# AdaLN, a selective scan and a mixture of experts in one kernel: fewer ScalarE and VectorE instructions per scan state, two more buffers, loads dealt out over other steps

## The reference, cut to what matters

```python
mod = (silu(c) @ wmod).reshape(4, 6, 1, 512)        # sa, ca, ga, sb, cb, gb; |ga|, |gb| kept >= 0.25
h = layernorm(x) * (1 + ca) + sa
x = x + ga * mamba(h)
h = layernorm(x) * (1 + cb) + sb
x = x + gb * moe(h)

def mamba(x):                                        # D = 512 channels, N = 16 states
    val, gate = split(x @ W_in)
    val   = silu(conv3(val))                         # depthwise, 3 taps
    Delta = softplus((val @ W_delta + delta_base) @ W_tau)
    dA    = Delta[..., None] * (-exp(A_log))
    A_bar = exp(dA)
    B_bar = expm1(dA) / (dA + 1e-6) * Delta[..., None] * (val @ W_B)[:, :, None, :]
    h_t   = A_bar_t * h_{t-1} + B_bar_t * val_t      # scan over the tokens
    y_t   = sum_n h_t * C_t                          # C = val @ W_C
    return (y * silu(gate)) @ W_out + x

def moe(x):                                          # 8 experts, hidden 256, top 2, and a shared one
    g = top2_normalized(sigmoid(x @ gate_W) * route_scale)
    return sum_e g_e * (gelu(x @ W1_e + b1_e) @ W2_e + b2_e) + shared(x)
```

## Time and profile before

| what | value |
|---|---|
| median of 3 runs | 4806.98 us (4793.49 to 4813.43) |
| the profiled execution | 4803.95 us, its span 4802.2 us |
| busy, share of the span | PE 81%, VectorE (DVE) 85%, ScalarE (ACT) 83%, GpSimd (POOL) 76% |
| mean share of the DMA engines' time: SyncE's queue, GpSimd's queue | 46.6%, 28.5% |

### The profile page before, as it was taken

The page is one execution under the profiler, slowest core; times in us unless marked ns, Lnnn a source line. Parts: engine busy times, 40 slices in busy tenths (PEclk is TensorE's granted clock), DMA queues, the critical chain, the costliest instruction groups (busy, mean ns, idle before and its releaser), DMA issues.

```text
span 4802.2 us, 37156 instructions
## 1 busy us (share of the span) xinstructions
PE 3874.3 (81%) x9708; PEld 1621.0 (34%) x9708; DVE 4088.0 (85%) x4054; ACT 4003.3 (83%) x4510; POOL 3648.1 (76%) x2308
## 2 busy tenths in 40 slices
PE   6623514989898888989898988899898977989889
PEld 3211201333333333333343333333333333333344
DVE  1398899999999999999999999999998998788830
ACT  1687889998999998999989998989899997978811
POOL 0399978887888888888878887888888886767621
PEclk8856756999999999999999999999999987989889
DMA  4678857878787978788787878887887885667542
GB/s 136 210 227 260 255 130 218 232 219 254 227 254 218 264 216 260 226 245 241 224 248 225 247 222 257 231 247 226 241 252 217 240 225 148 183 166 194 155 135 66
DMA packets 352222, 1037.19 MB, mean 216 GB/s; under 512 B 41254, under 2 KB 44390, under 8 KB 344711
## 3 DMA queue, kind: packets, MB, share of 16 engines
q1 hardware_dynamic: 278282, 766.35, 46.6%
q0 software_dynamic: 73728, 268.47, 28.5%
HBM read 639.74 MB, written 126.51 MB: 160 GB/s over the span
## 4 chain that ended last, share of the span: by engine, by line
PE 26%; ACT 23%; issue 15%; DVE 12%; DMA 12%; POOL 10%; SPq 0%; POOLq 0%; DVEq 0%; ACTq 0%
DMA ysum<-hs 9%; PE ps L1103 7%; PE ps L1122 6%; ACT inv L761 4%; PE ps L1073 3%; POOL inv L1377 3%; ACT inv L755 3%; DVE ps L1163 3%; DVE ps L1171 2%; DVE ps L1157 2%; ACT th L769 2%; ACT inv L766 2%; DVE hs L1191 2%; ACT abar L773 2%; PE ps L1047 2%
## 5 line engine op out<-in xcount | busy, mean ns | idle before, releaser
L1377 POOL TENSOR_TENSOR inv<-inv,th 128x1024 f32<-128x1024 f32 x512 | 1253.5, 2448 | 314.5 <-ACT th L769 314.4
L1103 PE MATMUL ps<-hf,w1r 128*128 128x512 f32 x2304 | 1115.0, 637 | 68.7 <-ACT xn L871 23.8
L1350 POOL TENSOR_TENSOR hs<-hs,Cb 128x1024 f32<-128x1024 f32 x384 | 962.3, 2506 | 54.0 <-DVE hs L1191 37.3
L1140 PE MATMUL ps<-Brow,pick 48*128 48x512 bf16 x1024 | 347.0, 423 | 593.4 <-DVE hs L1191 593.0
L1122 PE MATMUL ps<-w2r,hid 128*128 128x512 f32 x1776 | 816.1, 606 | 1.7 <-ACT xn L871 1.7
L1157 DVE TENSOR_TENSOR ps<-ps,us 128x1024 f32<-128x1024 f32 x512 | 628.3, 1227 | 193.7 <-PE ps L1140 193.3
L769 ACT ACTIVATE th<-delta,halfA 128x1024 f32<-128x1024 f32 (+1 forms) x640 | 606.3, 966 | 139.4 <-POOL inv L1377 139.3
L1191 DVE TENSOR_TENSOR_SCAN hs<-abar,carry,ps 128x512 f32<-128x512 f32 (+1 forms) x384 | 683.7, 1802 | 32.1 <-DMA ysum<-hs 32.0
L1171 DVE SCALAR_TENSOR_TENSOR ps<-ps,coef,inv 128x1024 f32<-128x1024 f32 (+1 forms) x640 | 674.3, 1072 | 25.9 <-POOL inv L1377 2.3
L1180 DVE SCALAR_TENSOR_TENSOR ps<-nrd,inv_kappa,ps 128x1024 f32<-128x1024 f32 (+1 forms) x640 | 675.3, 1073 | 16.1
L755 ACT ACTIVATE inv<-nrd,kappa 128x1024 f32<-128x1024 f32 (+1 forms) x640 | 577.0, 968 | 132.2 <-DVE ps L1171 132.1
(11 more groups left out here) (155 smaller groups left out, 5081.5 us busy)
## 6 DMA issues: line engine op xcount, KB each, us to landing
ysum<-hs POOLq DMA_DIRECT2D x512, 512.0 KB, 5.4
Cb<-c_rows SPq DMA_DIRECT2D x384, 512.0 KB, 4.5
w1r<-in_W SPq DMA_DIRECT2D x144, 512.0 KB, 5.5
w2r<-w_scaled SPq DMA_DIRECT2D x141, 512.0 KB, 6.7
Cb<-c_rows SPq DMA_DIRECT2D x128, 256.0 KB, 3.9
gbc<-expert_gates SPq DMA_DIRECT2D x128, 256.0 KB, 5.2
aw<-in_W_val SPq DMA_DIRECT2D x64, 256.0 KB, 6.0
xa<-in_x SPq DMA_DIRECT2D x32, 512.0 KB, 7.8
```

Source lines behind the costliest of these rows:

```text
L1103: mm = t.matmul(o, w1r[:, n % 2, k, h * P:(h + 1) * P], hf[:, k, :], start=(k == 0), stop=(k == G - 1))
L1350: gp_.tensor_tensor(hs[:, c % 3, :], hs[:, c % 3, :], Cb[:, c % 2, :], ALU.mult).then_inc(hC_done, 1)
L1377: gp_.tensor_tensor(inv[:, c % 6, :], inv[:, c % 6, :], th[:, c % 2, :], ALU.mult).then_inc(thinv_done, 1)
```

## The change

It (1) joins the four logarithms of a batch to two over [128, 2048], with the guard as a number in place of a column; (2) moves the coefficient of `times_weight` into the Exp of the inverse as a bias per partition (its logarithm), so that this Exp becomes two instructions in units of two halves while `times_weight` becomes one, with 1.0 as scalar; (3) writes `times_u` as a scalar_tensor_tensor; (4) takes the reciprocal standard deviations as Ln and Exp with a scale of -0.5 on ScalarE, at the places where these tables are already loaded, and drops Sqrt and reciprocal; (5) gives `hs` and `aw` a fourth buffer; (6) does the front's normalization, its statistics and transposes some steps earlier; (7) evicts two Delta products (`take_p` 2 and 3) in front of `times_ratio` at r = 11; (8) deals the loads of W2 (one expert a step: 12, 13, 15; 24, 25, 26; 30, 31, 0), W1 (7, 9; 25), h (r = 1), the aw weights and the h store (r = 29) over other steps. The last block keeps whole groups of W2.

```diff
-    AWB = 3
+    AWB = 4
-        hs = sb("hs", [P, 3, TB])
+        hs = sb("hs", [P, 4, TB])
...
-                done(v.reciprocal(coef[:], absA))
+                done(v.tensor_scalar(ln_coef[:], alog.rearrange("p g n -> p n g"), -2.0, math.log(DA_EPS), ALU.mult, ALU.add))
...
-            def load_w2(q, grp):
+            def load_w2(q, grp, members=(0, 1, 2)):
...
-                for p in GROUPS[grp]:
+                for p in [GROUPS[grp][m] for m in members]:
...
-            if r == 31:
-                load_aw(qn, 3)
...
+            if r == 2:
+                load_aw(qa, 7)
...
+            if r in (12, 13, 15) and qf != NQ - 1:
+                load_w2(qf, 0, ((12, 13, 15).index(r),))
             if r == 5:
-                load_w2(qf, 0)
                 if qf == NQ - 1:
+                    load_w2(qf, 0)
                     load_w2(qf, 1)
...
-            if r == 7:
-                load_aw(qa, 7)
+            if r in (7, 9):
+                load_w1(qf, (r - 7) // 2)
+            if r == 8:
                 load_aw(qa, 8)
-                load_w1(qf, 0)
-                load_w1(qf, 1)
-            if r == 8:
                 load_aw(qa, 9)
+            if r == 9:
                 load_aw(qa, 10)
-            if r == 9:
                 load_aw(qa, 11)
...
-            if r in (12, 17) and has(qn):
-                part = r // 17
+            if r in (12, 13) and has(qn):
+                part = r - 12
...
-            if r == 23:
-                load_w2(qf, 2 if qf == NQ - 1 else 1)
-            if r == 24:
+            if r == 23 and qf == NQ - 1:
+                load_w2(qf, 2)
+            if r in (24, 25, 26) and qf != NQ - 1:
+                load_w2(qf, 1, (r - 24,))
+            if r == 25:
                 load_w1(qf, 8)
...
-                    sp.wait_ge(st_h, 16 * (qx + 1))
-                    sp.dma_start(hf[:], h_d[qx]).then_inc(h_ld, 16)
+            if r == 1 and has(qf):
+                ge(sp, mm_w1, 2 * EX * qf)
+                sp.wait_ge(st_h, 16 * (qf + 1))
+                sp.dma_start(hf[:], h_d[qf]).then_inc(h_ld, 16)
             if r == 30:
                 load_gate_row(qf, 7)
-                if qf != NQ - 1:
-                    load_w2(qf, 2)
-            if r == 31:
+            if r == 29:
                 if has(qn):
                     sp.wait_ge(ev_t, G * (qn + 1))
                     sp.dma_start(h_d[qn], hTv).then_inc(st_h, 16)
+            if r in (30, 31) and qf != NQ - 1:
+                load_w2(qf, 2, (r - 30,))
+            if r == 0 and qp != NQ - 1:
+                load_w2(qp, 2, (2,))
...
-            def log(c):
-                act.wait_ge(sq_done, c + 1)
-                s.activation(inv[:, c % 6, :], inv[:, c % 6, :], ACT.Ln, bias=consts[:, 1:2]).then_inc(ln_done, 1)
+            def logs(c):
+                act.wait_ge(sq_done, c + 2)
+                two = flat(inv[:, c % 6:c % 6 + 2, :])
+                s.activation(two, two, ACT.Ln, bias=INV_GUARD).then_inc(ln_done, 2)
...
-                s.activation(inv[:, c % 6, :], inv[:, c % 6, :], ACT.Exp, scale=-1.0).then_inc(inv_done, 1)
+                for cols, g in parts(u):
+                    ins = s.activation(inv[:, c % 6, cols], inv[:, c % 6, cols], ACT.Exp, scale=-1.0,
+                                       bias=ln_coef[:, c % N, g:g + 1])
+                ins.then_inc(inv_done, 1)
...
             if w == 2:
-                if place == "start" and has(qf):
+                if place == "half logs" and has(qf):
                     act.wait_ge(f_stat, (TPB + 1) * (qf + 1))
-                    s.activation(rstdF[:, :, 0], momF[:, :, 1], ACT.Sqrt, bias=consts[:, 0:1]).then_inc(f_sqrt, 1)
+                    s.activation(rstdF[:, :, 0], momF[:, :, 1], ACT.Ln, bias=consts[:, 0:1]).then_inc(f_log, 1)
+                if place == 0 and has(qf):
+                    act.wait_ge(f_log, qf + 1)
+                    s.activation(rstdF[:, :, 0], rstdF[:, :, 0], ACT.Exp, scale=-0.5).then_inc(f_rstd, 1)
...
             if w == 5:
+                if place == "half logs" and has(qn):
+                    act.wait_ge(a_stat, (TPB + 1) * (qn + 1))
+                    s.activation(rstdA[:, :, 0], momA[:, :, 1], ACT.Ln, bias=consts[:, 0:1]).then_inc(a_log, 1)
+                if place == 0 and has(qn):
+                    act.wait_ge(a_log, qn + 1)
+                    s.activation(rstdA[:, :, 0], rstdA[:, :, 0], ACT.Exp, scale=-0.5).then_inc(a_rstd, 1)
             if w == 6:
                 if place == "start":
                     take_w1(qf, 6)
-                    if has(qn):
-                        act.wait_ge(a_stat, (TPB + 1) * (qn + 1))
-                        s.activation(rstdA[:, :, 0], momA[:, :, 1], ACT.Sqrt, bias=consts[:, 0:1]).then_inc(a_sqrt, 1)
...
-                if place == "squared" and has(qn):
+                if place == "squared":
+                    take_t(qn, (0, 1))
+                if place == "logs":
+                    take_t(qn, (2, 3))
+            if w == 5:
+                if place == 1 and has(qn):
                     act.wait_ge(a_rstd, qn + 1)
...
-                24: [("w1", qf, 13), ("w1", qf, 14)], 25: [("w1", qf, 15)], 26: [("w1", qf, 16), ("w1", qf, 17)],
-                27: [("t", qn, 0), ("t", qn, 1), ("w2", qf, 4)], 28: [("w2", qf, 5), ("t", qn, 2), ("t", qn, 3)], 29: [("w2", qf, 6)],
+                24: [("w1", qf, 13), ("w1", qf, 14)], 25: [("w1", qf, 15)] + [("t", qn, g) for g in range(G)], 26: [("w1", qf, 16), ("w1", qf, 17)],
+                27: [("w2", qf, 4)], 28: [("w2", qf, 5)], 29: [("w2", qf, 6)],
...
-                    v.tensor_tensor(X(c), X(c), us[:, u % 2, :], ALU.mult).then_inc(uB_done, 1)
+                    v.scalar_tensor_tensor(X(c), X(c), 1.0, us[:, u % 2, :], ALU.mult, ALU.mult).then_inc(uB_done, 1)
...
-                    for cols, g in parts(u):
-                        ins = v.scalar_tensor_tensor(X(c)[:, cols], X(c)[:, cols], coef[:, c % N, g:g + 1], inv[:, c % 6, cols],
-                                                     ALU.mult, ALU.mult)
-                    ins.then_inc(pw_done, 1)
+                    v.scalar_tensor_tensor(X(c), X(c), 1.0, inv[:, c % 6, :], ALU.mult, ALU.mult).then_inc(pw_done, 1)
...
-                    if c >= 3:
-                        dve.wait_ge(y_summed, 16 * (c - 2))
+                    if c >= 4:
+                        dve.wait_ge(y_summed, 16 * (c - 3))
...
+                if r == 11:
+                    take_p(qa, 2)
+                    take_p(qa, 3)
...
-                if r == 21 and has(qn):
+                if r == 16 and has(qn):
                     dve.wait_ge(ax_ld[0], 16 * (qn + 1))
                     tile_stats(xa, statsA, a_stat, (0, 1))
-                if r == 22 and has(qn):
+                if r == 17 and has(qn):
```

More of the change, by code:

```diff
@@ L1 @@
 from contextlib import ExitStack
+import math
 import numpy as np
@@ L97, in adaln_mamba_moe @@
         inv_kappa = sb("inv_kappa", [P, N, G])
-        coef = sb("coef", [P, N, G])
+        ln_coef = sb("ln_coef", [P, N, G])
         delta_lo = sb("delta_lo", [P, G])
         tau_bias = sb("tau_bias", [P, G])
-        consts = sb("consts", [P, 2])
+        consts = sb("consts", [P, 1])
         modc = sb("modc", [P, MODS * G, NB])
@@ L614, in sync_steps @@
             if r == 11:
-                load_aw(qn, 0)
-                load_aw(qn, 1)
-                load_aw(qn, 2)
+                for j in range(AWB):
+                    load_aw(qn, j)
             if r == 13:
@@ L801, in act_batch @@
             at("squared")
-            for c in states[0:2]:
-                log(c)
+            if states:
+                logs(c0)
             at("half logs")
-            for c in states[2:4]:
-                log(c)
+            if states:
+                logs(c0 + 2)
             at("logs")
@@ L953, in act_steps @@
                     ins.then_inc(a_xn, 1)
-                if place == 3:
-                    take_t(qn, (0, 1))
             if w == 7:
                 if place == "start":
-                    take_t(qn, (2, 3))
                     gelu(qf, 2)
@@ L986, in bank_held_to @@
                 return at + 1.95
-            held = {"t": (28.7, 28.7, 29.5, 29.5), "val": (1.5, 2.5, 3.5, 3.9), "gate": (8.3, 8.4, 9.5, 9.6), "p": (10.9, 11, 11.4, 11.5),
+            held = {"t": (26, 26.1, 26.4, 26.5), "val": (1.5, 2.5, 3.5, 3.9), "gate": (8.3, 8.4, 9.5, 9.6), "p": (10.9, 11, 11.4, 11.5),
                     "bc": (14.6,), "t2": (12, 12.1, 12.6, 12.7), "log": (14.95,), "gT": (15.9,),
@@ L1219, in mean_and_variance @@
                 ins.then_inc(sm, 1)
-            def rstd_of(rstd, sm):
-                v.reciprocal(rstd[:, :, 0], rstd[:, :, 0]).then_inc(sm, 1)
             def add_x1(kind, q, i, done, taken_):
@@ L1288, in late @@
                     take_p(qa, r - 9)
-                if r == 11:
-                    take_p(qa, 2)
-                    take_p(qa, 3)
-                if r == 25 and has(qn):
```

(9 more changed lines are left out.)

19 lines of the change are left out of this document (8 added, 11 removed).

## The result

The changed kernel takes 4858.89 us (median of 4 runs, 4855.09 to 4861.69), the kernel before 4806.91 us on the same chip: a ratio of 1.0109 (95% interval 1.0096 to 1.0121). It is 1.1% slower, where 4699 us was forecast. The profiled execution's span is 4858.3 us. Further down, one execution of e7 took 6053 us at a granted clock of 0.62, where its three others took 4698 to 4700 us at 0.89; it is left out of e7's number.

What follows compares the result with a forecast made beforehand. VectorE was taken as the bound, with three engines close behind. Savings of 41 + 40 + 45 less 35 us of new waits gave 91, plus 12 + 5 at the ends: 108 us off, so 4699 us, range 4635 to 4785.

Steps and rivals of the forecast that it cites:

- late loads: Rival: three late loads make TensorE wait some 4 us each, 12 us a window; slower, 4842 us; chance 0.07.
- the wait for B: VectorE waiting for TensorE's spread of B, twelve middle windows: 45 of 86.7 us would go, mainly at steps 27 and 28.
- VectorE's own work: Twelve middle windows: `times_weight` 29.6 us, `times_u` 7.3 and dropped reciprocals 3.9 less, together 41 us.
- the wait for y: VectorE's scan waiting for y's addition, middle windows: a fourth `hs` would remove 40 of 48.9 us.
- VectorE's waits for ScalarE and GpSimd: Middle windows: half of a 5.7 us a window difference in shrinkage taken as new VectorE waits, 35 us, bounds 0 and 70.
- Loads ... that cover it, and I cost it at nothing: Three loads one step ahead of use: TensorE waits 0 to 2 us, covered by its lead on VectorE; cost nothing.
- point of decision: The late-load rival was said to decide from some 3 us of TensorE waiting at each load.
- The objection to it: Against the late-load rival: W1, W2 and h are no longer sent in bursts of 1.5 to 2 MB.
- The table load: On ScalarE: a load costs 1.3 us by the trace; the skill's added 1380 ns drain was left out of the sum.
- `times_weight`: On VectorE: without its scalar column, 1285 ns becomes 1208, 77 ns a state, 29.6 us over 384 states.
- `times_u`: On VectorE: the new form goes from 1227 to 1208 ns, 7.3 us over 384 states.
- The logarithms: On ScalarE: two of 1137 ns become one of 1911, saving 363 ns each, 69.7 us over 192.

Runs made afterwards that it cites:

- e7: Changed kernel with W2 groups 1 and 2 loaded whole at steps 23 and 30, last W1 at 23, experts' deviation as before: 4698.40 us, 0.9786 of the kernel before.
- e1: Changed kernel with only the last expert's W1 load moved back from step 25 to step 24: 4818.07 us, 1.0027 of the kernel before.
- e11: e1 with group 1 of W2 loaded whole at step 23, group 2 still ending at step 0: 4819.81 us, 1.0027 of the kernel before.
- e2: e1 with W2 group 1 loaded whole at step 23 and group 2 whole at step 30: 4758.75 us, 0.9901 of the kernel before.
- e5: e2 with the experts' deviation as before, Sqrt at the start of batch 2 and a VectorE reciprocal: 4709.42 us, 0.9806 of the kernel before.
- e10: Changed kernel, late loads included, with only the experts' deviation back to Sqrt and reciprocal: 4802.06 us, 1.0000 of the kernel before.
- e6: e2 with the last expert's W1 loaded at step 23 instead of 24: 4752.17 us, 0.9893 of the kernel before.

## Why the prediction was wrong, step by step

The forecast gave 82% to faster and 7% to the rival that came true. That rival, late loads, was worked out at 4842 us; measured are 4859. It was at hand with its place and its price, and was turned down for a reason that does not hold.

The term of the sum that carried the failure is the wait for B. For the 384 states of the middle the forecast took 45 us off it; in the changed kernel it went from 86.7 to 195.7 us, 109 more. VectorE's own work fell by 32 us there (41 forecast), the wait for y by 48.9 (40), and VectorE's waits for ScalarE and GpSimd rose by 2 (35): late loads and a late deviation both reach VectorE as a late B.

**The step that failed: "Loads ... that cover it, and I cost it at nothing".** It set a landing time of 6.7 us against a step of 8.3 us, counted from the step in which the load stands in the program. But a queue in program order issues a load when it gets there. The changed kernel's trace has W1 issued at the moment at which TensorE is free for it (2058.38 and 2058.25), so the whole flight is waited for. Two of the three loads named cost 41 us (W1 at 25, e1) and 61 us (W2 at 0, e11 to e2); the third, W2 at 26, costs nothing (e11). The rows of before could have shown it: there W1, issued a step earlier, was already waited for 13 times, 20.9 us in all, and a step of advance taken from a load that is late is a step of waiting. The rival was right in kind and by parts in size: behind 3957 us it had +36 us, measured are 35, but for the middle its terms come to +11 us (57 + 35 - 41 - 40) and measured are 30. Its point of decision, some 3 us at each load, was passed at W1 alone (6.79 us here); for W2 at step 0 the changed kernel's TensorE waits 18.4 us in the middle stretch, 1.5 a window, and 3.3 once W1 is earlier (40.0 in e11). The objection to it, that smaller bursts land faster, was true and beside the point: the median w1r lands in 5.1 us where it took 5.5, w2r in 5.5 where it took 6.7, and the late W1 in 6.0 to 6.6 where it took 7.6 to 9.5.

**The second: new waits for ScalarE and GpSimd, taken at 35 us.** The text named the right place, GpSimd's normalization and all that queues behind it, but priced it as half of a balance between two engines' busy times. Nothing in that balance knows of an instruction order. It costs 49 to 57 us by itself (e5, e10), from 7.25 us of GpSimd idle a window (87.0 / 12), and little of it shows as VectorE waiting for ScalarE or GpSimd. The order of the program and durations like those in the earlier trace rows were enough to see it: a joined logarithm and a block of 1.9 us each, two table loads of 1.28 and three instructions of 1.13 to 1.15 us, that overlap a little, stand between the two small ones, 9.5 us in all.

**What was right.** With these edits mended, e7 takes 4698.40 us, the forecast's number. For the 384 states of the middle its terms are near the forecast's: VectorE's work 27 us less (41 forecast), the wait for y 49 less (40), the wait for B 52 less, from 86.7 to 34.5 (45), and VectorE's waits for ScalarE and GpSimd 36.5 more, from 5.1 to 41.6 (35). That is 94 us, and 91 were forecast; that they meet so closely is in part luck, as the terms miss by up to 14 us and cancel, and e7 is not the kernel that was forecast. VectorE is at 96.0% in the middle stretch, as written (3056.03 / 3182). The wait for B is 47.9 us in that stretch, where 42 was written. The table load has no drain.

**Terms that were mis-sized.** The y wait: it goes, but the fourth buffer by itself brings 15 to 20 us and not 40, since VectorE runs on into the waits for B and for ScalarE. `times_weight`: 59 ns less in place of 77, hence 22.7 us in place of 29.6 (384 x 59). `times_u`: nothing in place of 7.3. The logarithms: 1904 ns for 2048 elements, as forecast, but the old ones overlap each other: 548.0 us busy for 512 in the earlier trace rows are 1070 ns each and not 1137. The joined ones are 479.3 us for 256, 1872 each, so a pair saves 268 ns of ScalarE and not 363. The Exp with a column: 1142 where 1137 was taken. And ScalarE's drop is 16.4 us over the whole span (4003.3 to 3986.9), since the ends lose as forecast.

**What stays open.** e2 and e6 came out above what was expected of them; the deviation's idle time, still in both, is worth 49 us in e2. Of the 35 us lost in the three windows behind 3957 us, the loads are shown for the most part: they take 664 us in the changed kernel, 650 in e1, 647 in e11 and 627 in e2; but with only the deviation mended (e10) they still take 669. The fourth `aw` buffer with its moved loads, the earlier normalization of the front and the two earlier evictions at r = 11 were not tried apart; all three are in e7.

## What to carry to other kernels

Count the lead of a load from the moment at which its queue gets to issue it, which is when the instructions ahead of it in that queue have had their waits, and not from the step in which it stands; before moving it later, look in the trace at when it is issued and whether its user already waits. When a small value is moved to a point behind large work on another engine, ask who waits for it in order, and what stands behind that one. A buffer that removes a wait returns only the part that the next wait does not take.

## What the runs showed of the hardware

A scalar_tensor_tensor on 128x1024 with 1.0 as scalar takes 1226 to 1227 ns when its first operand is in PSUM, the same as the tensor_tensor that it replaces. `times_abar`, with `abar` first and the PSUM operand second, takes 1207. So the form of instruction by itself gains nothing. What makes the 20 ns is not shown: `times_abar` differs in the order of its operands and in its first operation, an addition where the others multiply, and no run changes one alone. With a column as scalar the order makes no such difference: `times_weight` before, PSUM first, takes 1285 ns, `times_ratio`, PSUM second, 1287.
